# Taking the context half of a second attention out of the first attention's loop: two units behind it, six behind the first experts

## The reference, cut to what matters

```python
x = x + L0_xattn(layernorm(x), ctx, ctx)      # softmax attention, 16 heads of 8
x = x + L0_ffn(layernorm(x))                  # 8 experts, top 2, 256 hidden
x = x + L1_xattn(layernorm(x), ctx, ctx)      # linear attention
x = x + L1_ffn(layernorm(x))                  # 8 experts, top 2, 512 hidden, and 2 shared ones

def L1_xattn(x, y):                           # y is the context, 32 x 77 x 128
    q = softmax(heads(x @ Wq.T + bq), axis=-1)
    k = softmax(heads(y @ Wk.T + bk), axis=-1)
    v = heads(y @ Wv.T + bv)
    D_inv = 1 / sum(q * sum(k, over tokens))
    kv = einsum('bhnd,bhne->bhde', k, v)      # needs the context alone
    out = q + (q @ kv) * D_inv
    return out @ Wp.T + bp
```

## Time and profile before

| | |
|---|---|
| median of 3 runs | 865.75 us |
| lowest and highest | 859.57, 866.41 us |
| the profiled execution | 863.05 us |
| its span, first to last instruction | 861.2 us |
| mean granted TensorE clock | 0.912 |
| busy: PE, DVE, ACT, POOL | 707.7, 423.4, 369.4, 398.0 us |

### The profile page before, as it was taken

The page is one execution under the profiler, slowest core; times in us unless marked ns, Lnnn a source line. Parts: engine busy times, 40 slices in busy tenths (PEclk is TensorE's granted clock), DMA queues, the critical chain, the costliest instruction groups (busy, mean ns, idle before and its releaser), DMA issues.

```text
span 861.2 us, 15400 instructions
## 1 busy us (share of the span) xinstructions
PE 707.7 (82%) x5064; PEld 509.6 (59%) x5064; DVE 423.4 (49%) x1184; ACT 369.4 (43%) x760; POOL 398.0 (46%) x490
## 2 busy tenths in 40 slices
PE   4999989989996139989971599999998899999930
PEld 2566666666665128877761455555553688888820
DVE  2476777778685324544434466666544122222223
ACT  2344444344442104334332366666653355555510
POOL 4122265465445725555562256565644145454430
PEclk9999999999997559999995599999999899999975
DMA  7521001101100166766633111000103566667537
GB/s 220 149 30 10 7 22 29 21 20 28 21 21 20 40 184 180 200 191 193 198 126 102 49 43 43 30 25 22 32 26 103 184 202 203 197 212 216 181 93 225
DMA packets 98870, 88.20 MB, mean 102 GB/s; under 512 B 49480, under 2 KB 82504, under 8 KB 98184
## 3 DMA queue, kind: packets, MB, share of 16 engines
q1 hardware_dynamic: 89704, 68.46, 29.6%
q0 software_dynamic: 9088, 18.76, 6.3%
HBM read 65.08 MB, written 24.83 MB: 104 GB/s over the span
## 4 chain that ended last, share of the span: by engine, by line
PE 62%; DVE 13%; POOL 7%; issue 6%; ACT 4%; DMA 4%; SPq 2%; POOLq 0%; DVEq 0%; ACTq 0%
PE pair L1134 24%; PE bank L1394 11%; PE bank L1134 7%; PE pair L1137 5%; PE bank L1137 5%; POOL xs_sorted L475 4%; PE bank L1237 3%; PE bank L1451 2%; DMA yg<-y_tok 2%; DVE sm L941 2%; PE bank L1252 2%; DVE smax L937 2%; ACT xa L576 2%; POOL rstd L462 1%; PE bank L1177 1%
## 5 line engine op out<-in xcount | busy, mean ns | idle before, releaser
L556 POOL DMA_INDIRECT y_tok<-ysb,xr x156 | 149.3, 957 | 161.1 <-DVE ysb L865 136.8
L475 POOL DMA_INDIRECT xs_sorted<-xa,slot_i x128 | 131.2, 1025 | 84.9 <-DVE slot_i L814 52.2
L1134 PE MATMUL pair<-xT,w_all 128*128 128x256 f32 x624 | 151.3, 386 | 6.7 <-DVE xT L850 4.1
L1134 PEld LDWEIGHTS pair<-xT,w_all 128*128 128x128 f32 x624 | 114.7, 194 | 22.2 <-DVE xT L850 5.0
L1394 PE MATMUL bank<-hT,w_all 128*128 128x256 f32 x468 | 114.0, 379 | 0.0
L865 DVE TENSOR_TENSOR ysb<-bank,xr 128x256 f32<-128x256 f32 x78 | 33.1, 424 | 129.7 <-PE bank L1137 129.7
L1394 PEld LDWEIGHTS bank<-hT,w_all 128*128 128x128 f32 x468 | 83.0, 190 | 8.1
L685 ACT ACTIVATE hT<-pair,w_all 128x256 f32<-128x256 f32 x156 | 65.4, 470 | 34.4 <-PE pair L1134 33.4
L693 ACT ACTIVATE yT<-bank,w_all 128x256 f32<-128x256 f32 x78 | 36.9, 473 | 87.5 <-PE bank L1394 86.4
L850 DVE COPY xT<-bank 128x256 f32<-128x256 f32 x78 | 32.7, 419 | 78.6 <-PE bank L1137 78.5
L937 DVE TENSOR_REDUCE smax<-pair 128x8 f32<-128x616 f32 x64 | 50.5, 788 | 41.8 <-PE pair L1134 41.3
(11 more groups left out here) (174 smaller groups left out, 1126.6 us busy)
## 6 DMA issues: line engine op xcount, KB each, us to landing
w_all<-in_w SPq DMA_DIRECT2D x39, 514.5 KB, 4.2
w_all<-in_w SPq DMA_DIRECT2D x39, 386.5 KB, 3.6
xr<-xs_sorted SPq DMA_DIRECT2D x78, 130.0 KB, 2.5
yg<-y_tok SPq DMA_DIRECT2D x32, 256.0 KB, 3.4
xs_sorted<-in_pads SPq DMA_DIRECT2D x30, 130.0 KB, 3.2
y_tok<-ysb,xr POOLq DMA_INDIRECT x156
xs_sorted<-xa,slot_i POOLq DMA_INDIRECT x128, 2.4
out<-x_sb SPq DMA_DIRECT2D x8, 256.0 KB, 2.4
```

Source lines behind the costliest of these rows:

```text
L475: g.indirect_dma_start(xs_dram[l], bass.IndirectOffsetOnAxis(ap=slot_i[:, i:i + 1], axis=0), xa[:, GT * c + j // TOPK, j % TOPK, :], None) ...
L556: g.indirect_dma_start(y_dram[l], bass.IndirectOffsetOnAxis(ap=xr[u % NXR][:, t, P:P + 1].bitcast(I32), axis=0), ysb[u % NYB][:, t, :], None)\
L1134: return mm(out_, l_, r_, start=True, stop=True)
```

## The change

All context work leaves the loop of `attention0` on all engines. A new function `contexts(part)` on PE, ACT and DVE does units 0 and 1 behind `attention0` (part 0) and units 2 to 7 behind `routed(0)` (part 1). Keys use banks 0 and 1 by turns, values banks 2 and 3, products banks 4 and 5. The scaling moves from POOL to DVE. `cxk` has no memory of its own any more: it is `hS[0:2]`. The waits that were there for the shared banks go, and new ones come in where the second attention first reads `kvm_all`, and before `routed(0)`.

```diff
+CX_EARLY = 2
+CX_PARTS = (range(CX_EARLY), range(CX_EARLY, NGRP))
...
+        cxk = hS[0:2]
...
-                    if live(v):
-                        context_scale(v)
...
+            def contexts(part):
+
+                for g in CX_PARTS[part]:
+                    context_values(g)
+                    context_exp(g)
...
             attention0()
+            contexts(0)
             routed(0)
+            contexts(1)
...
-            def context_sums(g):
+            def context_soft(g):
+                cx = heads(cxk[g % 2][0:NK, :])
                 dve.wait_ge(S("cx_exp"), g + 1)
                 after(dve, S("cx_soft"), g)
-                link(v.reduce_sum(cxm[0:NK, 1, :], heads(cxk[g % 2][0:NK, :]), AX.X))
-                v.reciprocal(cxm[0:NK, 2, :], cxm[0:NK, 1, :]).then_inc(S("cx_rec"), 1)
+                link(v.reduce_sum(cxm[0:NK, 1, :], cx, AX.X))
+                link(v.reciprocal(cxm[0:NK, 2, :], cxm[0:NK, 1, :]))
+                v.tensor_tensor(cx, cx, cxm[0:NK, 2, :].unsqueeze(2).to_broadcast([NK, GT * H, DH]), ALU.mult)\
+                    .then_inc(S("cx_soft"), 1)
...
+            def contexts(part):
+
+                gs = CX_PARTS[part]
+                for g in range(gs.start, gs.stop + 2):
+                    if g in gs:
+                        context_shift(g)
+                    if g - 1 in gs:
+                        context_soft(g - 1)
+                    if g - 2 in gs:
+                        context_kept(g - 2)
...
             def context_product(g):
                 pe.wait_ge(S("cx_soft"), g + 1)
-                after(pe, S("rdx_ready"), g)
-                after(pe, S("kvm_ready"), g)
+                pe.wait_ge(S("cx_v"), g + 1)
+                after(pe, S("kvm_ready"), g - 1)
...
+            def contexts(part):
+
+                gs = CX_PARTS[part]
+                if part == 0:
+                    pe.wait_ge(S("s_sub"), 2 * NT)
+                    pe.wait_ge(S("exp_done"), NG * NT)
+                    pe.wait_ge(S("bias_in0"), 32)
+                    pe.wait_ge(S("tails"), 1)
+                else:
+                    pe.wait_ge(S("h_ready"), NC0 * NB)
+                    pe.wait_ge(S("y_ready"), NB)
+                for g in range(gs.start, gs.stop + 1):
+                    if g in gs:
+                        context_keys(g)
+                        context_values(g)
+                    if g - 1 in gs:
+                        context_product(g - 1)
...
             attention0()
+            contexts(0)
             pe.wait_ge(S("emap"), 1)
             pe.wait_ge(S("bias1_ready"), 1)
+            pe.wait_ge(S("kvm_ready"), CX_EARLY)
             routed(0)
+            contexts(1)
             pe.wait_ge(S("ws_in"), 16)
```

More of the change, by code:

```diff
@@ L221, in build @@
         rdx = sb("rdx", [P, GT * P])
-        cxk = [sb(f"cxk{i}", [P, GT * P]) for i in range(2)]
         cxv = [sb(f"cxv{i}", [P, GT, NG, 33]) for i in range(2)]
@@ L975, in first_window @@
                         logits(v_ - 2)
-                    if s == 1 and live(v_):
-                        context_sums(v_)
                     if s == 2 and live(v_ - 2):
@@ L983, in second_window @@
                 def second_window(v_, s):
-                    if s == 0 and live(v_):
-                        context_shift(v_)
                     if s == 1 and live(v_ - 1):
                         output(v_ - 1)
-                    if s == 2 and live(v_):
-                        context_kept(v_)
                     if s == 2 and live(v_ - 2):
@@ L1162, in context_values @@
             def context_values(g):
-                pe.wait_ge(S("qT_ready"), g + 1)
+                after(pe, S("cx_v"), g - 1)
                 for t in range(GT):
                     at = (GT * g + t) * NK
-                    last = one(bank[7][0:NK, t * P:(t + 1) * P], ctx_all[:, at:at + NK], wv1)
+                    last = one(bank[2 + g % 2][0:NK, t * P:(t + 1) * P], ctx_all[:, at:at + NK], wv1)
                 last.then_inc(S("cx_vals"), 1)
             def context_keys(g):
-                pe.wait_ge(S("cx_v"), g + 1)
-                if g == 0:
-                    pe.wait_ge(S("bias_in0"), 32)
-                mm(bank[7][0:NK, :], ones_row[:, 0:NK], bias[0:1, 3, :].unsqueeze(1).to_broadcast([1, GT, P]),
+                after(pe, S("cx_sub"), g - 1)
+                mm(bank[g % 2][0:NK, :], ones_row[:, 0:NK], bias[0:1, 3, :].unsqueeze(1).to_broadcast([1, GT, P]),
                    start=True, stop=False)
@@ L1176, in context_keys @@
                     at = (GT * g + t) * NK
-                    last = mm(bank[7][0:NK, t * P:(t + 1) * P], ctx_all[:, at:at + NK], wk1,
+                    last = mm(bank[g % 2][0:NK, t * P:(t + 1) * P], ctx_all[:, at:at + NK], wk1,
                               start=False, stop=(t == GT - 1))
@@ L1187, in context_product @@
                         r = slice(32 * gr, 32 * gr + 32)
-                        last = one(bank[6][r, t * 33:(t + 1) * 33], cxk[g % 2][0:NK, t * P + 32 * gr:t * P + 32 * gr + 32],
-                                   cxv[g % 2][0:NK, t, gr, :])
+                        last = one(bank[4 + g % 2][r, t * 33:(t + 1) * 33],
+                                   cxk[g % 2][0:NK, t * P + 32 * gr:t * P + 32 * gr + 32], cxv[g % 2][0:NK, t, gr, :])
                 last.then_inc(S("kvp_done"), 1)
+            def contexts(part):
[14 more added lines that the diff above has]
+                        context_product(g - 1)
             def attention0():
@@ L1277, in keys @@
                 def keys(u):
-                    after(pe, S("cx_sub"), u)
+                    after(pe, S("qT_ready"), u)
                     if u == 0:
@@ L1306, in project @@
                     pe.wait_ge(S("o_ready0"), u + 1)
-                    after(pe, S("kvm_ready"), min(u + 2, NGRP))
                     for t in range(GT):
```

29 lines of the change are left out of this document (10 added, 19 removed).

## The result

| | before | after |
|---|---|---|
| median, 7 runs of each, one chip | 861.23 us | 870.98 us |
| lowest and highest | 859.04, 866.41 | 863.62, 874.76 |
| the profiled execution | 863.05 | 863.62 |
| its span, its mean clock | 861.2, 0.912 | 861.7, 0.912 |
| busy in it: PE, DVE, ACT, POOL | 707.7, 423.4, 369.4, 398.0 | 710.5, 429.1, 369.1, 389.6 |

After over before is 1.0099, with a 95% interval of 1.0054 to 1.0144: slower, by about 1%, where the forecast had 1.5% against the median shown.

The account below looks back on a forecast made before the run. The prediction took the first attention's loop as bound by PE in some places and DVE in others. Loop -22, early units +3.2 and late units +34.7 made +15.9 on 863.05, so 879 us, range 864 to 890.

Parts of the forecast that it names:

- What bounds a group: First attention's loop: PE bounds some places, DVE others; removing context work gains 2.7 us per group of four tiles.
- the zero for the fourth tile: Loop, fourth tile of a group: removing the context values' 1.0 us of PE gains 0, since the chain runs on DVE.
- Group 0: Loop's first group: would gain over 5 us, but transfers of attention 0's rearranged values cap it at some 2.3.
- The loop's term, -22: First attention's loop: 21.5 us from all groups plus 0.5 for the group missing a later one's moments, so -22 us.
- Six groups at 2.7: Loop: six of the groups each gain 2.7 us, the sum of 1.18, 0.39 and 1.09 by tile.
- the other-side rival: Loop PE-bound throughout: each group gives 4.7 us, 37 in all, total -6, 857 us; chance 15%.
- The early units: Units 0 and 1 between loop and first experts: delay the first expert transpose by +3 us (2.9 to 3.8).
- The late units: Six units before the second attention run serially, 5.90 to 8.11 us each: +28 to +41.4 us, middle +34.7 taken.
- the likeliest case: The forecast itself, whole kernel: +15.9 us, 879, with its own range of 874 to 884; chance 38%.
- Full clock in the late units: Rival: late units keep the full clock and cost +28, so +9.2 in all, 872 us; chance 25%.
- The loop loses its clock: Rival: PE idles more in the loop and half of the groups lose clock, +8 more, 885 or so; chance 10%.
- The half clock throughout: Rival: late units run at half clock throughout and cost +41.4, so +23.4 in all, 886 us; chance 12%.

Follow-up runs that it names:

- dummyv: After, with each next unit's context values also computed in the loop at their old place, into bank 7, read by nothing: 869.82 us, against 871.09 without.
- a_third: After unaltered, run again as the measure on the chip of early0, dummyv and tail4: 871.09 us, 1.0151 of before.
- early0: After with all eight context units behind the first experts and none before them: 881.19 us, 1.0237 of before.
- b_again: Before unaltered, run again on a second chip: 870.03 us, 0.997 of before.
- a_again: After unaltered, run again on a second chip: 887.45 us, 1.0165 of before.
- bfill: Before with the four products that spread the row sums done twice, in PE's 1.58 us wait: 870.21 us, 0.9968, against 876.41 for before unchanged.
- b_third: Before unaltered, the measure for bfill on its chip: 876.41 us, 1.003 of before.
- look2: After with each unit's product behind the keys and values of the second unit after it instead of the first: 874.72 us, 1.0004 of before.
- fill3: After with each late unit's values computed three times into the same bank, to fill PE's waits: 884.81 us, 1.0129 of before.
- tail4: look2 with four early units instead of two, their steps spread over waits in the loop's tail, and four late: 847.44 us, 0.9854 of before.

## Why the prediction was right in direction and too high

*What bounds a group.* Right. 2.7 forecast, 2.67 measured at full clock. Of its parts, the zero for the fourth tile was tested by itself (dummyv: 27.40). The split between the other three tiles was not tested apart.

*Group 0.* The cap by the values' DMA was there (the chain's 2.32 of DMA ahead of 34.37), and the weighted sums came 3.1 earlier, where 2.3 was forecast. To the first `rden` the gain was 5.4 on the first chip (59.95 to 54.53) and 3.9 on the second (58.09 to 54.16). The cap held for the start alone: from there to the first `rden` it was 22.5 us in before and 20.2 in after, so the later tiles gave their 2.3 in this group too, which the sum had left out. The next group gave 1.35 and 1.33, at a clock of 0.94 in after against 1.00 in before; in dummyv, at 1.00, it took 25.13 against 27.69, 2.6 less. The two together are 6.8 and 5.3 for a forecast of 5.0.

*The loop's term, -22, is the one that was mis-sized.* It measured -29.7 on the first chip and -25.7 on the second. The step that failed is "Six groups at 2.7": I took the price of a group at full clock and gave it to all of them, while four of them in the trace of before were not at full clock. Three gave 4.24, 5.89 and 4.24 us, 14.4 together, where the sum had 8.1, and the fourth (214.22 to 245.16, at 0.94) gave 4.7 where the sum had 3.2: 7.8 us more than forecast, which is clock that came back and as much as the 7.7 that were missed. The rest cancels. Group 0 and the one behind it gave 1.8 more than the sum had; the last group and the way to the loop's end gave 1.2 us where the sum had 3. The earlier trace rows had the 33.26 beside the 30.06, and the other-side rival says in its last sentence that half-clock stretches that fall on the keys vanish with them. That was the missing term, though only in part: three of the five low stretches stood on the keys, the two others on products that are still in the loop. Whether the clock came back because the keys were gone or because the wait of 1.58 us had shrunk to 0.45, no run separates, and before has one profile on its first chip. For this pair of profiles the sum would have come out with the gain taken from what each group took before, 31.6 - 27.4, 33.3 - 27.4, 31.6 - 27.4. On the second chip that rule gives too much: 23.1 us for the four middle groups, where 16.7 came, since after's groups lost the clock there too. The other side itself didn't happen. A group fell below 26 at full clock only where before's own was shorter (25.13 in dummyv against 27.69), and the price of a group was not all of PE's work in it.

*The early units.* Right, where it can be seen. From the end of the loop to the first expert transpose it was 12.21 us in before (304.15 to 316.36) and 15.68 in after (274.42 to 290.10): +3.5, forecast 3.2 with a range of 2.9 to 3.8; a_third against early0 gives 3.2. On the other chip it was 4.7 (13.14 in b_again, 17.83 in a_again), above the range. The stage's end moved by only 1.2 (after), 1.9 (a_again) and 2.2 (a_third), since the experts behind the transpose took 132.1 us in before and 129.8, 129.8 and 130.7 in these. Whether that is the change's doing stays open: with the same instructions the stage took 129.8 in bfill, 131.1 in b_third, 133.4 in dummyv and 134.2 in early0.

*The late units.* The mechanism was right at each step: one unit at a time, the product ahead of the next keys, PE waiting 1.76 us and more ahead of each product. The term, 34.7, measured 30.3 (after), 33.4 (a_third) and 35.8 (a_again), between the two ends of 28 and 41.4. look2 shows that the product's place makes the period, and that without it a unit takes 3.95, which is less than DVE's own 4.2 as I had summed it. fill3 shows the clock's share. The middle between the ends was a guess at the clock, and it came within 1.3 us of a_third and 1.1 of a_again, and 4.4 too high for the profiled execution of after.

*The sum.* With the measured terms of a_third: -29.7 + 2.2 + 33.4 + 0.8 = +6.7, where the forecast had -22 + 3.2 + 34.7 = +15.9. Of the 9.2 between them 7.7 is the loop, 1.0 the stage with the early units, 1.3 the late ones, and 0.8 goes the other way. The medians differ by 9.8. The 879 missed 870.98 by 8.0: 6.2 are the difference between 15.9 and 9.8, and 1.8 the start from one execution of 863.05, where the median of before came to 861.23. On the second chip the profiles give -25.7 + 1.9 + 35.8 + 0.9 = +12.9, and the loop is again the largest miss. The range of 864 to 890 held the 870.98, while the likeliest case's own range, 874 to 884, didn't.

*The rivals.* Full clock in the late units came near in time (872) with the wrong mechanism: the clock in the late part was 0.76 and 0.69, and the difference came from the loop. "The loop loses its clock" was the reverse of what the first chip did, where the loop gained clock; on the second chip after's groups at 0.89 took up to 3.0 more than 27.39, but before's had lost more. The half clock throughout didn't come: units of 8.92 and 7.97 us in a_again are followed by two of 6.80, so the sum that the prediction made by the Trainium skill's rule came out too high.

## What to carry to other kernels

Price the removal of work with two ends, and not by the one repetition that ran at full clock. The lower end is the gain at full clock. The upper end is what each repetition took before, minus the bound that is left: the losses of clock may go with the work. Here the upper end came on one chip (14.4 of 14.4 in three groups), and something between the two on another (16.7, between 10.7 and 23.1). Work that is moved to one place in a row needs its own schedule there: two banks of each kind did nothing while an in-order engine had to give out a unit's last step ahead of the next unit's first (6.3 to 8.9 us a unit, against 3.95 with the last step one unit later). And before it goes to a place of its own, put it into waits that are there: four units spread over the loop's tail cost the loop nothing, and with the later product that made the version of 847.44 us.

## What the runs showed of the hardware

The clock of TensorE in the same code was not the same from chip to chip: the changed loop's four middle groups are at 1.00 in after, a_third and tail4, and on the chip of a_again, look2 and fill3 two of the four are at 0.89 or 0.90 in each of the three profiles. The execution decides too: early0, on a_third's chip, had one of the four at 0.91. PE's waits in a_again's two slow groups, 3.0 and 2.5 us, are about those of after's groups at 1.00 (2.9). A wait of 1.43 us in each of after's middle groups left the clock at 1.00, while before lost it in a group whose waits are no longer than 1.58 and 0.73. So the waits alone don't tell where the clock falls, and I can't say what does: with the one wait filled (bfill) none of the four middle groups lost the clock behind it, and three stretches at half clock came at other places. Open too are groups longer than their neighbours at a clock of 1.00 (28.29 in a_again, 31.70 in bfill), and why one execution of after took 863.62 us and the six others 869.27 to 874.76.
